# Stage seams in a seven-stage kernel: earlier loads for the next stage, and weights laid out transposed

## The chip, the cores and the metric

The kernel runs as one launch on one core of one Trainium2 chip. The metric is the device time of an execution in microseconds (us). Engines are named as in the profile: PE (matmul), PEld (weight load of PE), DVE, ACT, POOL, SP (here only a queue that issues DMAs).

## The reference, cut to what matters

Two layers over x of 2 x 1024 tokens of width 512. Each layer norms x, computes an attention branch s and a gate branch g, and sets x = x + s * g.

```python
x = L0_attn_x
xn = _layernorm(x)
s = L0_attn(xn)          # qkv, two causal convolutions on q and on k, l2 norm, rope,
                         # 16 heads of 64 over 4 kv heads, causal softmax, times w_o.T
g = silu(L0_ffn(xn))     # relu^2 mlp + routed latent path, layer norm
x = x + s * g
xn = _layernorm(x)
s = L1_attn(xn)          # wq, wk, wv; rope; 32 heads of 16 over 8 kv heads; each query keeps
                         # the first 128 keys, its last 128 keys and its 8 best chunks of 16; times wo.T
g = silu(L1_ffn(xn))     # 8 low-rank experts: softmax(xn @ Wr.T + br), A then B
x = x + s * g
```

## The kernel before, in words

The program is seven stages, one after another, each a block of hand-written instruction streams for the engines with counting semaphores between them: gate, project, query, attend, middle, select, finish. At the end of a block all engines meet, and SP has first waited for its last stores; no instruction of the next block starts before that. A stage that needs its inputs at once therefore pays for the loads that it issues at its own start. Intermediate tensors (`q_parts`, `k_high`, `k_low`, `v`, `o0T`, `x1`, `o1`, `g`, `g1`) go through DRAM.

**Query** (`query_phase`). PE convolves, per block m of 128 output channels (8 blocks) and per chunk n of 512 tokens (4 chunks), 72 matmuls out of `conv_in` (a kept SBUF tensor of 65,664 bytes per partition) with fp16 weight parts that ACT and DVE make from float32 rows: DVE finds the extremes of the rows (`extremes`, L1041 to L1044), PE turns and spreads the peak (`find_peak` L876, `share_peak` L881), DVE scales, ACT and DVE write `c_wT` (L923, L1067). The rows of block 0, `rows0`, were loaded in the project stage. At the stage's start SP issues the loads of `k_in` and `raw1`, of the rows of block 1, and of seven small tables (`k_mean`, bias, `head_sum`, `head_spread`, cos, sin, temp; L812 to L818). PE, ACT, DVE and POOL each begin by waiting for all seven (`wait_ge(tables, 16 * 7)`). A chain of norms, rotation and splitting runs beside the convolution for ten units (two of k, eight of q); "hooks" place its PE steps (`sums` L847, `turn`, `back`, `spread`) inside the convolution. Only `sums` onwards, ACT's `offsets` and POOL's `rotate` read the tables. The unit of the last block runs alone at the end, and its four stores (L829) end the stage.

**Attend** (`attend_phase`) is the first layer's attention: 16 pairs of heads p = (g, b, i), g a kv group, b the batch, i a pair in it. SP issues three small tables (the last is `temp`), then `load(0, b)` for both b (q 1 MB, k_high, k_low and v 256 KB each, for each b), then the weights of the middle stage as rows (`MiddleWeights.load`). PE waits for the tables and for the four loads of its b. SP later issues `load(g + 1, b)` when group g is done with its buffers, and `store(p)` of each pair's 512 KB to `o0T`. Buffers `q`, `k_high`, `k_low`, `v` are the stage's own.

**Middle** (`middle_phase`) first has a small block of its own (`prep`): SP issues the loads of chunk 0 (`o_in` 2 MB, `g_in` and `x_in` 1 MB each) and of cos, sin (4 x 512 KB) and `br`; PE turns the weight rows by transposes in 17 groups (L1510), ACT and DVE copy them out (L1518, L1526). Then the main block: `project(c)` (L1630, 64 matmuls a chunk, 4 chunks of 512 tokens), and the rest of the layer's projections.

**Select** is the second attention; SP stores each group's result to `o1` in halves (`store(g, half)`, L2050), 16 groups g = (j, u) with u the batch, and preloads the finish stage's weight rows, `g_in` and `x_in` of two chunks (`FinishInputs`).

**Finish** (`finish_phase`): SP issues the loads of `o_in` of chunks 0 and 1 (L2460), PE turns the weight rows (L2484), ACT copies them (L2521), PE turns the tokens (`turn`, L2494) and multiplies (`project`, L2503), DVE gates and adds, SP stores and loads the chunk after next.

Of the kernel before, what the change touches and what calls it, by code (L numbers as in the profile page):

```python
# [704 lines left out]
def query_phase(nc, sem, dram, ident, half, conv_in, unscale, rows0, rows0_loaded):  # L705

    with ExitStack() as ctx:
# [97 lines left out]
        def _(sp):  # L805
# [34 lines left out]
        def _(pe):  # L840
            def sums(j):

                pe.wait_ge(square_ready, j + 1)
                if j > 0:
                    pe.wait_ge(rnorm_ready, j)
# [60 lines left out]
            pe.wait_ge(tables, 16 * 7)  # L906
# [9 lines left out]
        def _(act):  # L916
# [39 lines left out]
            act.wait_ge(tables, 16 * 7)  # L956
            weights(0)
            squares(0)
            offsets(0)
# [63 lines left out]
        def _(dve):  # L1023
            dve.wait_ge(tables, 16 * 7)

# [114 lines left out]
def attend_phase(nc, sem, dram, ident_bf, mask_kq, weights):  # L1140

    with ExitStack() as ctx:
# [7 lines left out]
        q = [sb(f"q{b}", [P, G0, S], FP16) for b in range(B)]  # L1150
        k_high = [sb(f"k_high{b}", [P, S], FP16) for b in range(B)]
        k_low = [sb(f"k_low{b}", [P, S], FP16) for b in range(B)]
        v = [sb(f"v{b}", [P, QT, HD0]) for b in range(B)]
# [19 lines left out]
        loaded = [sem(f"d_loaded{b}") for b in range(B)]  # L1173
# [25 lines left out]
        def _(sp):  # L1199
# [4 lines left out]
            def load(g, b):  # L1204
                sp.dma_start(q[b][:], dram["q_parts"][g * G0:(g + 1) * G0, :, b * S:(b + 1) * S].rearrange("h p t -> p h t")).then_inc(loaded[b], 16)
                for to, name in ((k_high, "k_high"), (k_low, "k_low")):
                    sp.dma_start(to[b][:], dram[name][g, :, b * S:(b + 1) * S]).then_inc(loaded[b], 16)
                sp.dma_start(v[b][:], dram["v"][b * S:(b + 1) * S, g * HD0:(g + 1) * HD0].rearrange("(n p) c -> p n c", p=P)).then_inc(loaded[b], 16)

# [5 lines left out]
            for b in range(B):  # L1215
                load(0, b)
            weights.load(sp)
            for p in range(ALL):
                g, b, i = where(p)
                if i == G0 // 2 - 1 and g + 1 < KV0:  # L1220
                    sp.wait_ge(pv_done, QT * (p + 1))
                    load(g + 1, b)
                if p >= 1:
                    store(p - 1)
            store(ALL - 1)
# [185 lines left out]
class MiddleWeights:  # L1411


    def __init__(self, ctx, nc, dram, sem):
        def raw(name, shape):
            return ctx.enter_context(nc.sbuf_tensor(f"e_w_{name}", shape, F32))

        self.dram = dram
# [1271 lines left out]
```

## Time and profile before

| | |
|---|---|
| median of 3 runs | 2838.74 us (2836.09 to 2839.36) |
| profiled execution | 2833.69 us, its span 2831.9 us |
| PE busy | 2417.7 us, 85% of the span |
| DVE, ACT, POOL busy | 1246.7, 940.6, 749.5 us |
| granted PE clock, mean | 0.94 of full speed |
| read from HBM, written | 127.05 MB, 60.29 MB |

The span is that of the first to the last instruction of one profiled execution; the execution's own time is 1.8 us longer, and the median of the runs shown is 5.05 us above that. Times below are counted from the span's start. "Idle before" is how long an engine did nothing before an instruction, with what ended it.

### The profile page before, as it was taken

The page shows a single profiled execution, that of the slowest core. Times are in us where ns is not written, and L with a number is a line of the kernel's source. Part 1 is how long each engine was busy: PE and PEld are TensorE (multiplying, and loading weights), DVE is VectorE, ACT ScalarE, POOL GpSimd, SP SyncE. Part 2 cuts the span into 40 slices and gives each one's busy share as a digit, 9 for nine tenths or more (in the row PEclk, how much of TensorE's full clock was granted, in tenths as well). Part 3 has the DMA queues.
Part 4 walks back from the last instruction along what each step waited for, and adds up shares of the span by engine and source line. Part 5 has one row for each costly group of instructions (what it writes and reads, how often), then busy time and mean ns, then how long its engine had stood idle before and what let it go on. Part 6 is the DMA issues. An engine that isn't in the chain of part 4 may idle for free. (4 is left out here: it accounts for less than half of the span.)

```text
span 2831.9 us, 46056 instructions
## 1 busy us (share of the span) xinstructions
PE 2417.7 (85%) x19426; PEld 1159.1 (41%) x19426; DVE 1246.7 (44%) x2617; ACT 940.6 (33%) x1597; POOL 749.5 (26%) x749
## 2 busy tenths in 40 slices
PE   7999859999788999999499976888578888888766
PEld 3444334444333444443255543444233333333333
DVE  2332231100043333321287772444487877787602
ACT  1111120100021111110377750222257676767630
POOL 0111001110235222223344430222343333333300
PEclk9999979999889999999699988999789999999988
DMA  6000010000222111000422204331553553444122
GB/s 215 30 30 30 15 67 15 26 26 19 101 64 63 38 41 49 16 15 16 128 83 83 83 31 163 121 121 62 112 132 60 77 75 59 59 77 75 28 93 91
DMA packets 132462, 190.33 MB, mean 67 GB/s; under 512 B 45016, under 2 KB 67288, under 8 KB 130848
## 3 DMA queue, kind: packets, MB, share of 16 engines
q1 hardware_dynamic: 130144, 183.20, 24.8%
q8 instruction: 153, 2.51, 0.4%
q10 hardware_dynamic: 2112, 4.19, 0.4%
q14 instruction: 53, 0.43, 0.1%
HBM read 127.05 MB, written 60.29 MB: 66 GB/s over the span
## 5 line engine op out<-in xcount | busy, mean ns | idle before, releaser
L896 PE MATMUL c_ps_c<-conv_in,c_wT 128*128 128x512 f16 x2304 | 508.4, 380 | 2.6 <-DVE c_wT L1067 2.6
L2219 ACT ACTIVATE f_probs<-f_ps_s 128x512 f32<-128x512 f32 x576 | 321.5, 596 | 136.9 <-PE f_ps_s L2123 55.6
L2337 DVE TENSOR_REDUCE f_chunk_max<-f_ps_a 128x64 f32<-128x1024 f32 x320 | 321.8, 1033 | 92.1 <-PE f_ps_a L2090 50.8
L896 PEld LDWEIGHTS c_ps_c<-conv_in,c_wT 128*128 128x128 f16 x2304 | 222.6, 98 | 279.6 <-issue 13.5
L2123 PE MATMUL f_ps_s<-f_qs,f_ks 128*32 128x512 bf16 x2304 | 218.4, 387 | 64.1 <-ACT f_probs L2219 55.5
L2090 PE MATMUL f_ps_a<-f_ka,f_qa 128*32 128x512 bf16 (+3 forms) x3072 | 200.3, 339 | 47.1 <-DMA f_v_all<-v 21.4
L1325 ACT ACTIVATE d_probs<-d_ps_s,d_shift 128x512 f32<-128x512 f32 (+3 forms) x384 | 196.5, 583 | 82.5 <-PE d_ps_s L1264 72.8
L2145 PE MATMUL f_ps_o<-f_probs,f_v 128*32 128x512 f32 (+3 forms) x1536 | 151.8, 493 | 25.7 <-ACT f_probs L2219 25.6
L624 PE MATMUL b_ps<-b_xb,b_wT 128*128 128x512 f32 x320 | 140.5, 600 | 18.0 <-DMA b_xb<-xnT 18.0
L1259 PE MATMUL d_ps_s<-d_q,d_k_high 128*64 128x512 f16 (+3 forms) x768 | 125.7, 328 | 33.0 <-DMA d_v<-v 33.0
L1275 PE MATMUL d_ps_o<-d_probs,d_v 128*64 128x512 f32 (+3 forms) x768 | 146.0, 488 | 0.0
L2211 ACT ACTIVATE f_qs<-f_ps_t 32x512 bf16<-32x512 f32 x192 | 112.6, 586 | 100.2 <-PE f_ps_t L2105 97.3
L2090 PEld LDWEIGHTS f_ps_a<-f_ka,f_qa 128*32 128x32 bf16 x3072 | 75.5, 98 | 164.2 <-issue 61.9
L2277 POOL TENSOR_SCALAR f_absent<-f_rest 128x576 f32<-128x576 f32 x32 | 54.3, 1697 | 332.2 <-DVE f_rest L2354 332.2
L1630 PE MATMUL e_ps_s<-e_oT,e_o_in 128*128 128x512 f32 x256 | 115.7, 614 | 21.8 <-DMA e_x_in<-in_x 21.8
L2123 PEld LDWEIGHTS f_ps_s<-f_qs,f_ks 128*32 128x32 bf16 x2304 | 59.5, 96 | 163.7 <-ACT f_probs L2219 135.4
L1392 DVE RECIPROCAL d_inverse<-d_ps_n 128x1024 f32<-128x1024 f32 x16 | 104.9, 6558 | 44.7 <-PE d_ps_n L1286 44.7
L1264 PE MATMUL d_ps_s<-d_q,d_k_low 128*64 128x512 f16 (+3 forms) x384 | 124.3, 328 | 0.0
L1263 PE MATMUL d_ps_s<-d_q,d_k_low 128*64 128x512 f16 (+3 forms) x384 | 124.3, 328 | 0.0
L189 PE MATMUL a_ps_m<-a_xnT,a_up 128*128 128x512 f32 x256 | 112.3, 599 | 2.5 <-ACT a_relu L236 2.5
L207 PE MATMUL a_ps_d<-a_down,a_hidden 128*128 128x512 f32 x256 | 112.5, 592 | 0.0
L1032 DVE SCALAR_TENSOR_TENSOR c_raw<-c_ps_c,c_w_unscale,c_offset 128x512 f32<-128x512 f32 x32 | 24.0, 751 | 192.8 <-PE c_ps_c L896 192.8
(282 smaller groups left out, 3689.9 us busy)
## 6 DMA issues: line engine op xcount, KB each, us to landing
f_qa<-qk SPq DMA_DIRECT2D x96, 128.0 KB, 3.7
f_qs<-qk SPq DMA_DIRECT2D x96, 128.0 KB, 4.5
d_q<-q_parts SPq DMA_DIRECT2D x8, 1024.0 KB, 5.4
o0T<-d_stage SPq DMA_DIRECT2D x16, 512.0 KB, 2.6
e_o_in<-o0T SPq DMA_DIRECT2D x4, 2048.0 KB, 10.8
qk<-e_part SPq DMA_DIRECT2D x12, 640.0 KB, 4.9
rows<-in_qc_w SPq DMA_DIRECT2D x4, 1536.0 KB, 7.1
c_rows<-in_qc_w SPq DMA_DIRECT2D x4, 1536.0 KB, 7.7
```

Of the source, the lines that this page charges most:

```text
L624: last = pe.matmul(out[:], wT[:, k, u * P:(u + 1) * P], x[:, k, 1:], start=(k == 0), stop=(k == KD - 1))
L896: last = pe.matmul(ps_c[n % 2][:], wT[m % 2][:, w, i * TAPS + a, :], conv_in[:, x, i, b, h * CH + a:h * CH + a + CH], start=(i == 0 and a ...
L1259: pe.matmul(out[sides[e], lo - low:], k_high[b][:, keys[e]], q[b][:, h, lo:hi], start=True, stop=False)
L1263: pe.matmul(out[sides[0], lo - low:], k_low[b][:, keys[0]], q[b][:, h, lo:hi], start=False, stop=True)
L1264: pe.matmul(out[sides[1], lo - low:], k_low[b][:, keys[1]], q[b][:, h, lo:hi], start=False, stop=True)\
L1275: last = pe.matmul(ps_o[a * HD0:(a + 1) * HD0, lo:hi], v[b][:, kt, :], probs[n % RING][a][:, lo:hi], start=(kt == 0), stop=((kt + 1) * P = ...
L1325: act.activation(probs[n % RING][SCORES[c][1]][:, lo:hi], ps_s[c % BANKS][:, lo - hi + CH:], ACT.Exp, bias=shift[:, 0:1], scale=HD0 ** -0. ...
L2090: last = pe.matmul(out[side(e), h, 0:w], qa[u][:, 2 * p + h, side(e, qt * P)], ka[u][:, kh * CH:kh * CH + w], start=True, stop=not last_keys)
L2123: last = pe.matmul(out[side(e), :], ks[u][:, side(e, kt * P)], qs[u][version][:, :, at:at + P], start=True, stop=not (masked or part))
L2145: last = pe.matmul(ps_o[2 * HD1 * h:2 * HD1 * (h + 1), lo - half * CH:], v[u][:, kt, :], probs[m % HELD][:, h, lo - half * CH:], start=(kt ...
L2219: act.activation(probs[m % HELD][:, :, at:at + P], ps_s[n % 2][:].rearrange("p (h n) -> p h n", n=P), ACT.Exp, scale=HD1 ** -0.5).then_inc ...
L2337: dve.tensor_reduce(chunk_max[:, qt - 2, :, at:at + w // CHUNK], src.rearrange("p h (c k) -> p h c k", k=CHUNK), AX.X, ALU.max).then_inc(a ...
```

## The change: what it does

1. **Query stage, table waits.** DVE's wait for the seven tables is gone. PE waits for them in `sums(0)`, ACT after `weights(0)` and `squares(0)`. POOL waits as before.
2. **First attention's loads.** A new `AttendInputs` lays q, k_high, k_low, v of both b out in the first 28,672 bytes per partition of `conv_in`. In the query stage SP, at the last unit, waits for all convolutions and for the stores of the units before, issues the eight loads of group 0, and then stores the last unit. Attend issues none for group 0.
3. **Middle weights.** The host lays `w_o`, `wq`+`wk`, `wv`+`lora_a`+`lora_r`, `lora_b` out transposed. Attend's SP loads them straight into `oT`, `qkT`, `tokT`, `bT`, and cos, sin, `br` with them. The `prep` block, with its transposes and copies, is gone.
4. **Middle's first tokens.** `o_in`, `g_in`, `x_in` lie in another part of `conv_in`; attend's SP issues the loads of chunk 0 between the last but one and the last store, after a wait for the stores of pairs 0 to 13.
5. **Finish.** `wo` comes transposed by the host, the four groups of transposes and the copies are gone. The loads of `o1` for chunks 0 and 1 are issued in the select stage, in its last group before `store(g, 0)`, after a wait for all stores up to group 14.

```diff
@@ query_phase
                 if j + 2 < MQ:
                     sp.wait_ge(w_ready, PIECES * (j + 1))
                     load_rows(j + 2)
+                if j == UNITS - 1:
+                    sp.wait_ge(conv_done, NCH * MQ)
+                    sp.wait_ge(stored, stored_by(j))
+                    for b in range(B):
+                        attend_inputs.load(sp, 0, b)
                 store(j)
@@ sums
                 pe.wait_ge(square_ready, j + 1)
+                if j == 0:
+                    pe.wait_ge(tables, 16 * 7)
@@ tensor
-            pe.wait_ge(tables, 16 * 7)
             pe.wait_ge(cleared, 2)
@@ scalar
-            act.wait_ge(tables, 16 * 7)
             weights(0)
             squares(0)
+            act.wait_ge(tables, 16 * 7)
             offsets(0)
@@ vector
-            dve.wait_ge(tables, 16 * 7)
...
+class AttendInputs:
+    def __init__(self, dram, sem, space):
+        flat = space[:].rearrange("p a m b n -> p (a m b n)")
+        G0 = H0 // KV0
+        sizes = [G0 * S] * B + [S] * B + [S] * B + [2 * QT * HD0] * B
+        parts = [flat[:, sum(sizes[:i]):sum(sizes[:i + 1])] for i in range(len(sizes))]
...
+    def load(self, sp, g, b):
+        sp.dma_start(self.q[b], dram["q_parts"][g * G0:(g + 1) * G0, :, b * S:(b + 1) * S].rearrange("h p t -> p h t")).then_inc(self.loaded[b], 16)
+        for to, name in ((self.k_high, "k_high"), (self.k_low, "k_low")):
+            sp.dma_start(to[b], dram[name][g, :, b * S:(b + 1) * S]).then_inc(self.loaded[b], 16)
+        sp.dma_start(self.v[b], dram["v"][b * S:(b + 1) * S, g * HD0:(g + 1) * HD0].rearrange("(n p) c -> p n c", p=P)).then_inc(self.loaded[b], 16)
@@ attend_phase, sync
-            for b in range(B):
-                load(0, b)
             weights.load(sp)
             for p in range(ALL):
...
+            for i in range(2):
+                sp.wait_ge(stored[i], 16 * (ALL // 2 - 1))
+            weights.load_tokens(sp, 0)
             store(ALL - 1)
@@ MiddleWeights.load
-        sp.dma_start(self.o_rows[:], dram["w_o"].rearrange("(o p) c -> p o c", p=P)).then_inc(self.loaded, 16)
...
+        sp.dma_start(self.oT[:], dram["w_oT"].rearrange("(m p) d -> p m d", p=P)).then_inc(self.w_loaded, 16)
+        sp.dma_start(self.qkT[:].rearrange("p i k n -> p (i k n)"), dram["qk1_wT"]).then_inc(self.w_loaded, 16)
+        sp.dma_start(self.tokT[:].rearrange("p k t -> p (k t)"), dram["tok_wT"]).then_inc(self.w_loaded, 16)
+        sp.dma_start(self.bT[:], dram["lora_bT"]).then_inc(self.w_loaded, 16)
+        for b in range(B):
+            sp.dma_start(self.cos[:, b, :], dram["cos1"]).then_inc(self.tables, 16)
+            sp.dma_start(self.sin[:, b, :], dram["sin1"]).then_inc(self.tables, 16)
+        sp.dma_start(self.br[:], ...).then_inc(self.tables, 16)
+
+    def load_tokens(self, sp, c):
+        sp.dma_start(self.o_in, self.dram["o0T"][:, :, ds(c * CH, CH)].rearrange("m p t -> p m t")).then_inc(self.loaded, 16)
+        sp.dma_start(self.g_in, tokens("g")).then_inc(self.loaded, 16)
+        sp.dma_start(self.x_in, tokens("x")).then_inc(self.loaded, 16)
@@ middle_phase
-        with ExitStack() as prep:
...      (the whole prep block: loads of chunk 0 and of cos, sin, br; 17 groups of transposes; 17 copies)
@@ middle_phase, project
+                if c == 0:
+                    pe.wait_ge(weights.w_loaded, 64)
                 pe.wait_ge(loaded, 48 * (c + 1))
@@ select_phase, sync, in the loop over g
+                if g == GROUPS - 1:
+                    for half in range(2):
+                        sp.wait_ge(o_stored[half], 16 * (GROUPS - 1 + 1))
+                        inputs.load_heads(sp, half, half)
                 store(g, 0)
@@ FinishInputs, finish_phase
-        sp.dma_start(self.w_rows[:], self.dram["wo"].rearrange("(o p) c -> p o c", p=P)).then_inc(self.w_loaded, 16)
+        sp.dma_start(self.wT[:], self.dram["wo"].rearrange("(k p) d -> p k d", p=P)).then_inc(self.w_loaded, 16)
-            for u in range(2):
-                load(u, u)
-            for k in range(KO):
-                for o in range(D // P):
-                    last = pe.transpose(ps_t[k % 4][:, o * P:(o + 1) * P], w_rows[:, o, k * P:(k + 1) * P], ident[:])
-                last.then_inc(w_turned, 1)
-            for k in range(KO):
-                act.wait_ge(w_turned, k + 1)
-                act.activation(wT[:, k, :], ps_t[k % 4][:], ACT.Copy).then_inc(w_ready, 1)
```

## Rows read from the trace of the kernel before

**Rows 1.** The page's first part, busy time of PE and others.

```profile
PE 2417.7 (85%) x19426; PEld 1159.1 (41%) x19426; DVE 1246.7 (44%) x2617; ACT 940.6 (33%) x1597; POOL 749.5 (26%) x749
```

**Rows 2.** Waits of PE: us in total, times, longest us.

```profile
PE c_ps_x L876 <- DVE c_ends L1044: 38.7, 3, 28.2
PE d_ps_s L1259 <- DMA d_v<-v: 33.0, 1, 33.0
...
PE e_psw L1510 <- PEq L1142: 11.0, 1, 11.0
```

**Rows 3.** Timeline, project to query: start us, us, what [idle before].

```profile
761.61 0.20 POOL L985 MEMSET c_ones<- 1x128 f32 x1 [33.63 <-POOLq L384]
...
773.21 0.44 SPq L818 DMA_DIRECT2D c_temp<-in_key_temp  x1
779.38 3.35 DVE L1041 TENSOR_REDUCE c_ends<-rows 128x1 f32<-128x3072 f32 x1 [29.05 <-DMA c_temp<-in_key_temp]
...
790.47 9.89 PE L896 MATMUL c_ps_c<-conv_in,c_wT 128*128 128x512 f16 x36 [2.60 <-DVE c_wT L1067]
...
795.81 2.37 POOL L998 TENSOR_TENSOR c_turned<-c_k_in,c_cos 128x1024 f32<-128x1024 f32 x1 [33.42 <-DVE c_swapped L1076]
...
800.29 1.07 PE L847 MATMUL c_ps_n<-c_square,c_head_sum 128*32 128x512 f32 x8
```

**Rows 4.** Timeline, the first convolution block.

```profile
803.19 7.96 PE L896 MATMUL c_ps_c<-conv_in,c_wT 128*128 128x512 f16 x36
...
812.21 5.45 POOL L1007 TENSOR_TENSOR c_rnorm<-c_norm,half 128x32 f32<-128x32 f32 x1 [2.35 <-DVE c_norm L1080]
```

**Rows 5.** Timeline, query to attend.

```profile
1336.15 0.75 DVE L1032 SCALAR_TENSOR_TENSOR c_raw<-c_ps_c,c_w_unscale,c_offset 128x512 f32<-128x512 f32 x1 [12.62 <-PE c_ps_c L896]
...
1368.66 0.45 SPq L829 DMA_DIRECT2D q_parts<-c_high  x1
...
1376.15 0.42 SPq L1202 DMA_DIRECT2D d_temp<-in_key_temp  x1
...
1378.98 0.15 DVE L1354 TENSOR_SCALAR d_minus<-d_temp 128x1 f32<-128x1 f32 x1 [10.35 <-DMA d_temp<-in_key_temp]
...
1384.91 0.64 PE L1259 MATMUL d_ps_s<-d_q,d_k_high 128*64 128x512 f16 x2 [33.03 <-DMA d_v<-v]
```

**Rows 6.** Timeline, attend to middle.

```profile
1681.47 14.06 SPq L1213 DMA_DIRECT2D o0T<-d_stage  x2
...
1693.96 1.22 DVE L1397 TENSOR_TENSOR d_stage<-d_o_raw,d_inverse 128x1024 f32<-128x1024 f32 x1
1698.24 0.37 SPq L1470 DMA_DIRECT2D e_o_in<-o0T  x1
...
1698.30 5.67 PE L1510 MATMUL e_psw<-ident,e_w_o 128*128 128x128 f32 x32 [10.98 <-PEq L1142]
...
1711.55 29.43 PE L1630 MATMUL e_ps_s<-e_oT,e_o_in 128*128 128x512 f32 x64 [3.60 <-DMA e_x_in<-in_x]
```

**Rows 7.** The page's DMA issues: KB each, median us to landing.

```profile
o0T<-d_stage SPq DMA_DIRECT2D x16, 512.0 KB, 2.6
```

**Rows 8.** Timeline, middle's second chunk: a store and the loads behind it.

```profile
1742.46 0.38 SPq L1597 DMA_DIRECT2D x<-e_x  x1
...
1759.18 30.01 PE L1630 MATMUL e_ps_s<-e_oT,e_o_in 128*128 128x512 f32 x64 [18.20 <-DMA e_x_in<-in_x]
```

**Rows 9.** Timeline, select to finish.

```profile
2688.74 0.42 DVE L2382 TENSOR_TENSOR f_o_out<-f_ps_t,f_inverse 128x256 f32<-128x256 f32 x1
```

**Rows 10.** Timeline, start of the finish stage.

```profile
2721.69 3.65 PE L2484 MATMUL h_ps_t<-ident,h_w_rows 128*128 128x128 f32 x16 [3.47 <-PEq L1857]
...
2727.23 6.60 PE L2494 MATMUL h_ps_t<-ident,h_o_in 128*128 128x128 f32 x32 [1.90 <-DMA h_o_in<-o]
```

**Rows 11.** Windows: us, busy of PE, PEld, DVE, ACT, POOL, granted clock, DMA share, GB/s.

```profile
786.00:791.00 5.00, 1.69 (x6) 0.87 (x7) 2.43 (x7) 2.57 (x4) 0.00 (x0) 0.50 0.00 0
...
2730.00:2735.00 5.00, 5.00 (x25) 4.28 (x24) 0.00 (x0) 3.48 (x6) 0.00 (x0) 0.68 0.01 3
```

More of the change, by code:

```diff
@@ L702, in _, with query_phase @@
                         take(dve, b, h, u).then_inc(took_dve, 1)
-def query_phase(nc, sem, dram, ident, half, conv_in, unscale, rows0, rows0_loaded):
+def query_phase(nc, sem, dram, ident, half, conv_in, unscale, rows0, rows0_loaded, attend_inputs):
     with ExitStack() as ctx:
@@ L1149, in attend_phase @@
         LATE = S - KT_POOL * P
[L1150 to L1153, printed above, removed]
+        q, k_high, k_low, v, loaded, load = inputs.q, inputs.k_high, inputs.k_low, inputs.v, inputs.loaded, inputs.load
         ones = sb("ones", [P, HD0])
@@ L1411, with __init__, sb @@
 class MiddleWeights:
[L1414 to L1425 removed]
+    def __init__(self, ctx, nc, dram, sem, space, used):
+        def sb(name, shape):
+            return ctx.enter_context(nc.sbuf_tensor(f"e_{name}", shape, F32))
+        KV1D = KV1 * HD1
+        self.TOK = KV1D + HL * RL + HL
+        self.NQK = D // P + KV1D // P
+        flat = space[:].rearrange("p a m b n -> p (a m b n)")
+        sizes = [2 * MQ * CH, 2 * TT * D, 2 * TT * D]
+        o_in, g_in, x_in = [flat[:, used + sum(sizes[:i]):used + sum(sizes[:i + 1])].bitcast(F32) for i in range(3)]
+        self.dram = dram
+        self.o_in = o_in.rearrange("p (m t) -> p m t", t=CH)
+        self.g_in = g_in.rearrange("p (t d) -> p t d", d=D)
+        self.x_in = x_in.rearrange("p (t d) -> p t d", d=D)
+        self.oT = sb("oT", [P, MQ, D])
+        self.qkT = sb("qkT", [P, self.NQK, KD, P])
+        self.tokT = sb("tokT", [P, KD, self.TOK])
+        self.bT = sb("bT", [P, OL])
+        self.br = sb("br", [P, HL])
+        self.cos = sb("cos", [P, B, S])
+        self.sin = sb("sin", [P, B, S])
+        self.w_loaded = sem("e_w_loaded")
+        self.loaded = sem("e_loaded")
+        self.tables = sem("e_tables")
@@ L1462, in middle_phase @@
-        o_in = sb("o_in", [P, MQ, CH])
-        loaded = sem("e_loaded")
+        oT, qkT, tokT, bT, br, cos, sin = weights.oT, weights.qkT, weights.tokT, weights.bT, weights.br, weights.cos, weights.sin
+        o_in, g_in, x_in, loaded, load, tables = weights.o_in, weights.g_in, weights.x_in, weights.loaded, weights.load_tokens, weights.tables
         def tokens(name):
             return dram[name].rearrange("(c t p) d -> c p t d", t=TT, p=P)
-        def load(sp, c):
-            sp.dma_start(o_in[:], dram["o0T"][:, :, ds(c * CH, CH)].rearrange("m p t -> p m t")).then_inc(loaded, 16)
-            sp.dma_start(g_in[:], tokens("g")[ds(c, 1)].rearrange("a p t d -> p (a t) d")).then_inc(loaded, 16)
-            sp.dma_start(x_in[:], tokens("x")[ds(c, 1)].rearrange("a p t d -> p (a t) d")).then_inc(loaded, 16)
@@ L2435, in finish_phase @@
         KO = H1 * HD1 // P
-        w_rows, g_in, x_in, loaded = inputs.w_rows, inputs.g_in, inputs.x_in, inputs.loaded
-        wT = sb("wT", [P, KO, D])
-        o_in = [sb(f"o_in{i}", [P, TT, KO * P]) for i in range(2)]
+        wT, o_in, g_in, x_in, loaded = inputs.wT, inputs.o_in, inputs.g_in, inputs.x_in, inputs.loaded
         oT = [sb(f"oT{i}", [P, KO, CH]) for i in range(2)]
@@ L2458, in _ @@
         def _(sp):
-            def load(c, u):
-                sp.dma_start(o_in[u][:], tokens(dram["o1"])[ds(c, 1)].rearrange("a p t d -> p (a t) d")).then_inc(loaded[u], 16)
             def store(c, u):
```

127 lines of the change are left out of this document (36 added, 91 removed).

## The prediction

> **What bounds the kernel now.** I read the page first: PE is busy for 85% of the span [rows 1], no other engine for half of it. So inside a stage PE sets the pace, and 414 us are left in which it does nothing. The list of what PE waited for says where [rows 2]: long single waits, each at the start of a stage, and not many small ones. Every stage begins after all engines met, so such a wait shifts everything behind it and is paid in full. Then I read the timeline around each seam that the diff touches, to see which arrival ends the wait and what would end it if that arrival were gone. The gate stage and the seams gate to project and middle to select aren't touched. In a seam the test for each saved microsecond is: what is the next thing that PE has to wait for?
>
> **Seam 1, project to query.** The block opens at 761.61 (POOL's memset). DVE's first reduction starts at 779.38, released by the load of `temp`, the last of seven tables, issued at 773.21 [rows 3]. That reduction reads only `rows0`, which was loaded in the stage before. With the wait gone it starts with the block, at about 761.65: 779.38 - 761.65 = 17.7 us. From there the chain is the old one (two reductions, peak, scale, `c_wT`), 790.47 - 779.38 = 11.1 us long, and PE's first convolution starts at 772.8 instead of 790.47.
>
> Who still needs the tables? They land at 779.4 as before, since SP's queue is the same there. PE meets them in `sums(0)`, which stood 800.29 - 790.47 = 9.8 us behind the first convolution [rows 3], so at 782.6: 3.2 us after they land. It doesn't wait. ACT waits before `offsets(0)` from some 776 to 779.4; the offsets are needed by DVE's `take(0, 0)` only after 72 matmuls. Queued behind that wait is `sums_out(0)`, which can't start before `sums(0)` is done anyway. POOL's `rotate(0)` started at 795.81, i.e. would start at 778.1, and now starts at 779.4, 1.3 us late against PE. Behind it is POOL's `invert(0)`, before which POOL sat idle for 2.35 us [rows 4]; the 1.3 us go into that. So nothing of 17.7 is given back. The early squares on ACT need only `k_in` and `raw1`, issued first.
>
> PE starts cold either way: the granted clock is 0.50 at 786 to 791 [rows 11], that is 1.2 GHz, and its idle stretch only shrinks from some 32 to some 15 us. Were the clock to stay up I would gain what separates the first 36 matmuls, 9.89 us [rows 3], from the next 36, 7.96 us [rows 4]: 1.9 us. I count nothing and keep it for the upper bound. Seam 1: **17.7 us, 16.5 to 19.6**.
>
> **Seam 2, query to attend.** The last convolution ends at 1336.1 and the last unit's chain of ACT, DVE, POOL and small PE steps runs to 1368.66, where its stores start [rows 5]. The eight new loads are issued when the convolution is done; SP has nothing else to do for those 32 us, and 3.5 MB need some 12 us at the rate of seam 3. They are long there when the block ends. The wait for stores of earlier units holds nothing up, for these stores belong to a unit whose chain ran during the last block of convolutions. The tail itself isn't shortened: it is bound by its chain. In the new block PE waited for `v`'s load to 1384.91; the next thing it needs is the three tables, and DVE's first instruction shows that `temp`, the last, is there at 1378.98 [rows 5]. Saving: 1384.91 - 1378.98 = **5.9 us, 5.4 to 6.5**. ACT's table load and first exponential hang on PE's first score and move with it. The weights of the middle stage are now 4 MB of longer runs and 2 MB of cos and sin, on SP's queue from 1376.6; nobody reads them for 300 us, and SP's next duty, `load(1, 0)`, comes after a pair's values, some 40 us later. Nothing.
>
> **Seam 3, attend to middle.** PE began the middle stage at 1698.30 with the transposes and reached `project(0)` at 1711.55, released by the load of `x_in` [rows 6]. Removed: 68 transposes, 17 copies, one meeting of the engines, and the wait for 4 MB. If tokens and weights are there, `project(0)` takes the place of the transposes at 1698.30: 13.25 us.
>
> But the token loads are 4 MB, issued after `store(14)` at 1681.47 [rows 6], and `store(15)` is issued behind them. DVE's last product starts at 1693.96 and takes 1.22 us [rows 6], so `store(15)` is issued at 1695.2. Do the loads get out of its way? The nearest row: behind a 1 MB store issued at 1742.46, the same three loads released PE at 1759.18 [rows 8], so 5 MB in 16.7 us, 300 GB/s with the start-up in it. Here 0.5 + 4 MB = 4.7 million bytes need 15.7 us, from 1681.5 to 1697.2. A store to `o0T` lands 2.6 us after its issue [rows 7], so `store(15)` at 1697.8; with 0.5 MB behind the loads it lands at 1697.2 + 1.7 = 1698.9. The seam ends 1.1 us later (bounds: 0 if the loads run faster, 4 if they run at 250 GB/s). A second small loss: PE enters `project(0)` after 11 us of idleness, where it had warmed up in the transposes. The 64 matmuls took 29.43 us there and 30.01 us after an 18 us wait [rows 6, 8]: 0.6 us. Seam 3: 13.25 - 1.1 - 0.6 = **11.6 us, 8.5 to 13.3**. After it the middle stage is the old one: its chunks load each other through the same queue and the same single buffers.
>
> Here a rule of the Trainium skill speaks against the change, "DMA: Bandwidth & Descriptors", section "Queues, rings and completion order": each DMA engine takes descriptors in ring order, and the copies of one issuing engine share those rings, so a store issued behind 4 MB of loads waits for them. No row of before has a store behind loads with its landing in view. The Trainium skill's table in the same page's section "Bandwidth" has 16 MB at 425 GB/s; as an estimate from that Trainium skill page 4.7 million bytes would be through in 11.1 us, before `store(15)` is issued, and the 1.1 us would be nothing (total 41.8 instead of 40.7).
>
> **Seam 4, select to finish.** The half `(14, 1)` is written by DVE at 2688.74 [rows 9], stored right away, and landed some 2.6 us later; then the two loads of `o1`, 2 MB, have 30 us until the finish stage. Queued behind SP's new wait are the two last stores, whose data come 10 us and more later. So they aren't held up. The finish stage starts at 2721.69 with PE's transposes of weights; `turn(0)` started at 2727.23, released by the load of `o_in` [rows 10]. It takes their place: 2727.23 - 2721.69 = **5.5 us, 4.5 to 6**. PE is cold in either case (clock 0.68 for 2730 to 2735, rising some 6 us after the turns began [rows 11]), so the turns take their 6.6 us again. From there each chunk waits for the store and loads of the one before, as now. The four copies on ACT (L2521) lay beside PE: nothing.
>
> **Sum.** 17.7 + 5.9 + 11.6 + 5.5 = 40.7 us, against the profiled execution 2833.69 - 40.7 = 2793.0 us (span 2791.2). The median of the runs shown is 5.05 us above the profiled execution, and the result is a median too: 2838.74 - 40.7 = **2798.0 us**.
>
> **Rivals.**
>
> *Rival A, the token loads eat their own gain.* Loads and `store(15)` share one queue; if the loads run at half the 300 GB/s (they read `o0T` in 1024 runs of 2 KB while DMA also writes), they land at 1713, later than now: seam 3 costs 2 us, total 27, time 2811.7. Against it: the same loads, with a larger store in front, ran at 300 [rows 8]. 5%. The Trainium skill's ring-order rule, "DMA: Bandwidth & Descriptors", "Queues, rings and completion order", is the same mechanism for the store behind them.
>
> *Rival B, a second wait in the query stage takes the place of the first.* In the first block PE already waited three times for DVE's extremes, 38.7 us in all, of which 28.2 are the seam [rows 2]. If the early start leaves ACT or POOL, which still wait for the tables, on the chain that feeds the second and third extremes, up to the 3.4 us (ACT) or 1.3 us (POOL) come back, and if rows of block 1, landing about 770 to 774, were late for DVE, a little more. With 3.4 us given back the total is 37.3, the time 2801.4. 12%.
>
> *Rival C, a larger gain:* the clock stays up or rises sooner at the seams now that PE idles less (seam 1 by 1.9, seam 3 by 2), total 44.6, time 2794.1. For it: shorter idle stretches. Against it: the shortest of them, before the finish stage, is 3.5 us [rows 10] and the clock there is low [rows 11]. 10%.
>
> *Rival D, the other side: the attention loop gets slower.* Its q, k, v now lie in `conv_in`, at other addresses, from which PE reads every score and value. The loop lasts 1698.3 - 1384.9 = 313 us with PE busy nearly throughout. From 13% longer PE instructions on (40.7 / 313) it takes all the gain back; at 16%, 50 us, the time would be 2848. For it: nothing that the trace shows; no row tells an operand's address. 2%.
>
> *Rival E, the loads are hidden anyway,* that is, the inferred releasers are wrong and the seams are set by the meeting of engines: then seams 1 and 4 give 0 and the total is 17.5, time 2821.2. Against it: POOL runs at the block's opening, 17.7 us before DVE, and PE transposes 5.5 us before its turn. 3%.
>
> **How the numbers follow.** The forecast with its bounds has 68%, A 5, B 12, C 10, D 2, E 3. The four seams' bounds add up to 34.9 and 45.4 us: 2803.8 and 2793.3. They hardly all fall on one side, but the runs themselves spread by 2.7 us below and 0.6 above their median, and a median of another set can move as much. I take 2789 to 2808, which also holds B and C and leaves out A, D and E, 10%, and some of the rest. A measurement of this kernel can tell a change from none at about 0.2%, 5.7 us. Only D ends slower: 2%, and 1 more for the unforeseen; within 0.2%: 1%; faster: 96%.
>
> **What would show it.** Right: DVE's first reduction of the query stage at the block's opening, and PE's first convolution 11 us later; no wait of PE at the first `sums`; PE's first score of attend some 3.7 us after the block's first POOL instruction, released by `temp`'s tables; `project(0)` of the middle stage within 2 us of the block's opening, the block itself opening 1.1 us later after DVE's last product than now (4.3 us); `turn(0)` as PE's first work in the finish stage. Wrong: the third wait for extremes in the query stage longer than now; attend's loop not 313 us; the span from the last product to `project(0)` above 8 us.

## The result, and the profile after

The changed kernel takes 2793.87 us (median of 4 executions, 2788.19 to 2863.77), the kernel before 2837.58 us in the same set: 43.7 us less, ratio 0.9839 with a 95% interval of 0.9814 to 0.9864. One of the four executions, the one of 2863.77 us, ran at a lower granted clock (0.902, the others 0.941 to 0.948) and is left out of the ratio, and the median of the other three is 2789.5 us, 48.1 less and only just inside the forecast range. Forecast were 2798.0 us, 40.7 us less, in a range of 2789 to 2808. A later set of five runs of the same kernel gave 2793.95 us against 2837.69 us, ratio 0.9846 (0.9833 to 0.986). The profiled execution took 2789.5 us, its span is 2787.7 us.

First the busy times from the page of the changed kernel.

```profile
PE 2398.0 (86%) x19342; PEld 1143.3 (41%) x19342; DVE 1241.4 (45%) x2609; ACT 932.8 (33%) x1584; POOL 750.5 (27%) x749
```

PE is busy for 19.7 us less [rows 1]: 13.3 us of that are the 68 + 16 transposes that are gone. The other 6.4 lie mostly in stages that the change doesn't touch, and are scatter: a second profile of the same kernel has PE busy for 2405.9 us. The span is 44.2 us shorter, so somewhat more than half of it was idle time of PE. The list of PE's waits says which (us in total, times, longest us):

```profile
PE h_ps_t L2451 <- DMA h_o_in<-o: 29.0, 2, 14.5
...
PE d_ps_s L1278 <- DMA d_temp<-in_key_temp: 27.0, 1, 27.0
...
PE c_ps_x L883 <- DVE c_ends L1048: 20.9, 3, 10.5
...
PE e_ps_s L1595 <- DMA conv_in<-in_x: 17.2, 1, 17.2
...
PE e_ps_s L1595 <- DVEq L55: 11.2, 1, 11.2
...
PE h_ps_t L2451 <- ACTq L55: 3.6, 1, 3.6
```

Against [rows 2]: the wait for DVE's extremes fell by 17.8 us, and PE's first score of attend is released by `temp` and no longer by `v`. Two releasers are new, `DVEq L55` and `ACTq L55`: L55 is the line of `primed`, with which an engine opens a stage (it sets the semaphores' starting values). At these two seams PE now waits for nothing but the opening of the stage. The two 14.5 us waits inside finish stayed, and so did the wait for chunk 1 in middle, 17.2 us (18.2 before).

The timeline of the changed kernel at the first seam:

```profile
759.20 0.20 POOL L991 MEMSET c_ones<- 1x128 f32 x1 [33.62 <-POOLq L384]
759.24 3.35 DVE L1045 TENSOR_REDUCE c_ends<-rows 128x1 f32<-128x3072 f32 x1 [11.31 <-PEq L384]
...
770.27 10.49 PE L903 MATMUL c_ps_c<-conv_in,c_wT 128*128 128x512 f16 x36 [2.54 <-DVE c_wT L1071]
...
778.38 2.38 POOL L1004 TENSOR_TENSOR c_turned<-c_k_in,c_cos 128x1024 f32<-128x1024 f32 x1 [18.39 <-DMA c_temp<-in_key_temp]
...
780.69 1.06 PE L854 MATMUL c_ps_n<-c_square,c_head_sum 128*32 128x512 f32 x8
...
792.48 5.45 POOL L1013 TENSOR_TENSOR c_rnorm<-c_norm,half 128x32 f32<-128x32 f32 x1
```

DVE starts 0.04 us after the block opens, where it started 17.77 us after [rows 3]. PE's first `sums` shows no wait. POOL's 2.35 us of idleness before `invert(0)` [rows 4] is gone. Counted from DVE's first reduction, `rotate(0)` starts 19.14 us behind it instead of 16.43, so 2.7 us late, and `invert(0)` 33.24 instead of 32.83: the idleness took up all but 0.4 us. At the other three seams:

```profile
1316.79 0.38 SPq L1162 DMA_DIRECT2D conv_in<-q_parts  x1
...
1359.31 0.64 PE L1278 MATMUL d_ps_s<-conv_in 128*64 128x512 f16 x2 [26.99 <-DMA d_temp<-in_key_temp]
...
1655.93 0.32 SPq L1231 DMA_DIRECT2D o0T<-d_stage  x1
...
1656.36 0.37 SPq L1473 DMA_DIRECT2D conv_in<-o0T  x1
...
1668.42 1.22 DVE L1416 TENSOR_TENSOR d_stage<-d_o_raw,d_inverse 128x1024 f32<-128x1024 f32 x1
1669.67 0.33 SPq L1231 DMA_DIRECT2D o0T<-d_stage  x1
1672.93 29.51 PE L1595 MATMUL e_ps_s<-e_oT,conv_in 128*128 128x512 f32 x64 [11.15 <-DVEq L55]
...
2680.84 0.42 DVE L2351 TENSOR_TENSOR f_o_out<-f_ps_t,f_inverse 128x256 f32<-128x256 f32 x1
...
2684.06 5.07 PE L2451 MATMUL h_ps_t<-ident,h_o_in 128*128 128x128 f32 x32 [3.62 <-ACTq L55]
```

`project(0)` follows DVE's last product by 4.51 us, where the transposes followed it by 4.34 and `project(0)` by 17.59 [rows 6]. `turn(0)` follows DVE's last output of select by 3.22 us. Laid end to end, the two profiles give this ledger (a piece is the difference of two starts):

| piece | before | after | gain |
|---|---|---|---|
| to the opening of query (nothing changed there) | 761.61 | 759.20 | 2.41 |
| opening to DVE's first reduction | 17.77 | 0.04 | 17.73 |
| to the end of the convolution | 556.77 | 557.55 | -0.78 |
| tail of query to the opening of attend | 39.15 | 38.97 | 0.18 |
| opening to PE's first score | 9.61 | 3.55 | 6.06 |
| attention loop to DVE's last product | 309.05 | 309.11 | -0.06 |
| last product to `project(0)` | 17.59 | 4.51 | 13.08 |
| middle and select to DVE's last output | 1007.07 | 1007.91 | -0.84 |
| last output to `turn(0)` | 8.61 | 3.22 | 5.39 |
| turns, products, the rest | 104.67 | 103.64 | 1.03 |

The sum is 44.2 us, the difference of the spans. The four seams hold 42.3 of it. The first line is luck of that execution: over the 13 profiles of this study the query block opened between 759.2 and 764.5 us, the stretch from DVE's first reduction to the end of the convolution lasts 556.8 to 559.6 us, and the line of middle and select lies between 1004.3 and 1014.6 us in the twelve of them that load middle's chunks as these two kernels do. That is why the experiments are read seam by seam, from starts inside one profile, and only then by their times.

### The profile page after: what moved, and what is told of

The parts are those of the page before. It is cut to its first block and busy times, and to the rows that moved or that the text cites. A ratio compares the mean times of both kernels' runs of the same rounds, so it can differ in the third digit from the quotient of the medians.

```text
span 2787.7 us, 45851 instructions
## 1 busy us (share of the span) xinstructions
PE 2398.0 (86%) x19342; PEld 1143.3 (41%) x19342; DVE 1241.4 (45%) x2609; ACT 932.8 (33%) x1584; POOL 750.5 (27%) x749
## 5 line engine op out<-in xcount | busy, mean ns | idle before, releaser
L1278 PE MATMUL d_ps_s<-conv_in 128*64 128x512 f16 (+3 forms) x768 | 125.6, 329 | 27.0 <-DMA d_temp<-in_key_temp 27.0
L2180 ACT ACTIVATE f_qs<-f_ps_t 32x512 bf16<-32x512 f32 x192 | 112.7, 587 | 103.8 <-PE f_ps_t L2074 101.0
L1294 PE MATMUL d_ps_o<-d_probs,conv_in 128*64 128x512 f32 (+3 forms) x768 | 146.0, 488 | 0.0
L1595 PE MATMUL e_ps_s<-e_oT,conv_in 128*128 128x512 f32 x256 | 115.9, 615 | 28.3 <-DMA conv_in<-in_x 17.2
L1282 PE MATMUL d_ps_s<-conv_in 128*64 128x512 f16 (+3 forms) x384 | 124.2, 328 | 0.0
L1283 PE MATMUL d_ps_s<-conv_in 128*64 128x512 f16 (+3 forms) x384 | 124.2, 328 | 0.0
```

The lines of the kernel that those rows point to most:

```text
L1278: pe.matmul(out[sides[e], lo - low:], k_high[b][:, keys[e]], q[b][:, h, lo:hi], start=True, stop=False)
L1282: pe.matmul(out[sides[0], lo - low:], k_low[b][:, keys[0]], q[b][:, h, lo:hi], start=False, stop=True)
L1283: pe.matmul(out[sides[1], lo - low:], k_low[b][:, keys[1]], q[b][:, h, lo:hi], start=False, stop=True)\
L1294: last = pe.matmul(ps_o[a * HD0:(a + 1) * HD0, lo:hi], v[b][:, kt, :], probs[n % RING][a][:, lo:hi], start=(kt == 0), stop=((kt + 1) * P = ...
```

## The experiments

Each is the changed kernel with one edit undone, unless it says otherwise. Reference values are those of the changed kernel: 2793.95 us in its second set.

### The table waits undone

```diff
+            pe.wait_ge(tables, 16 * 7)     # head of PE's stream; the one in sums(0) is gone
+            act.wait_ge(tables, 16 * 7)    # ahead of weights(0)
+            dve.wait_ge(tables, 16 * 7)    # head of DVE's stream
```

> The changed kernel with one part undone: PE, ACT and DVE wait for the seven tables at the head of the query stage again. My theory (the seam's gain is the wait for the last table and nothing else): from the block's opening to DVE's first reduction 17.8 us instead of 0.04, everything behind it as late, time 17.7 us above the changed kernel, about 2811.5 us. Rival (part of the gain was luck of the run or a shorter warm-up of PE after the shorter idle stretch): 15 to 16 us, the convolution's first 36 matmuls faster or slower than 10.5 us.

Measured: 2813.65 us (median of 4), ratio to the kernel before 0.992 (0.9905 to 0.9935), 19.7 us above the changed kernel. The timeline at DVE's first reduction and PE's first convolution; the block opened at 762.60:

```profile
780.16 3.35 DVE L1046 TENSOR_REDUCE c_ends<-rows 128x1 f32<-128x3072 f32 x1 [28.83 <-DMA c_temp<-in_key_temp]
...
791.25 9.63 PE L901 MATMUL c_ps_c<-conv_in,c_wT 128*128 128x512 f16 x36 [2.60 <-DVE c_wT L1072]
```

17.56 us are back, released by `temp`. The first 36 matmuls take 9.63 us after the long idle stretch and 10.49 after the short one: the start isn't warmer (9.85 to 10.57 us in the ten profiles with the short stretch, 9.63 to 10.28 in the three with the long one). The theory stands: the wait is back at nearly its full length and not at the rival's 15 to 16 us. That the matmuls differ from 10.5 us, as the rival had it, has the sign opposite to a warm-up. The medians differ by 2.2 us more than the seam (19.7 against 17.5), which the scatter of the untouched stretches covers: the span of this profile is 17.2 us above that of the second profile of the changed kernel (2811.8 and 2794.6 us).

### Attend's loads of group 0 back in attend

```diff
-                if j == UNITS - 1:           # query: wait, then attend_inputs.load(sp, 0, b)
...
+            for b in range(B):               # attend, before weights.load(sp)
+                load(sp, 0, b)
```

> The changed kernel with the eight loads of group 0 issued by SP at the head of the attend stage again, still into the space of conv_in. My theory: PE's first score comes 9.6 us after POOL's first instruction of the block instead of 3.55, released by v's load; 6.1 us more, about 2800 us; the attention loop itself lasts 313.4 us as in both kernels. Rival (the place of q, k and v in conv_in matters to PE): the loop's length differs between kernels with and without it; this run has it in conv_in, and its loop would then differ from the one of before.

Measured: 2800.72 us, 6.8 us above the changed kernel; ratio to before 0.988 (0.9863 to 0.9896). The block opened at 1360.72:

```profile
1371.07 0.64 PE L1275 MATMUL d_ps_s<-conv_in 128*64 128x512 f16 x2 [33.78 <-DMA conv_in<-v]
```

10.35 us from the opening, 6.8 more than in the changed kernel. The loop from PE's first score to DVE's last product takes 309.10 us here and lies between 309.04 and 309.13 in all 13 profiles, two of which (the kernel before and the one with tokens only) have q, k and v in buffers of their own. Where PE reads them from makes no difference.

### Seam 3, its two halves apart

Tokens late, weights transposed:

```diff
-            weights.load_tokens(sp, 0)       # attend, before the last store
...
+            load(sp, 0)                      # middle, SP's first instruction
             store_x1(0)
```

> The changed kernel with the token loads of chunk 0 issued at the head of the middle stage; weights still arrive transposed, so there is no prep block. Theory T (the token loads set the seam, the transposes lay hidden under them): project(0) starts 12 to 13.5 us after the stage opens, the whole 13.1 us of seam 3 are lost, about 2806 us. Theory W (the transposes set the seam, the loads only their last 3.6 us): about 4 us are lost, 2798 us.

The kernel before with tokens early, weights as rows:

```diff
+            for i in range(2):               # attend, before the last store
+                sp.wait_ge(stored[i], 16 * (ALL // 2 - 1))
+            weights.load_tokens(sp, 0)
             store(ALL - 1)
...
-                    load(sp, 0)              # prep block of middle
```

> The kernel before with one thing changed: o_in, g_in and x_in of chunk 0 are loaded into buffers of their own by SP between the last but one and the last store of attend; rows of weights, prep block, transposes and copies as before, cos, sin and br at the head of the middle stage. Theory T, with the transposes next in line (9.7 us of PE plus the meeting at the block's end): project(0) starts about 10.5 to 11 us after the stage opens instead of 13.25, gain 2.5 us against before, 2835 us. Theory W' (loads are all of it, the transposes cost nothing even uncovered): gain 13 us, 2824.5 us. If T holds here and in the run with late tokens, neither half of seam 3's edit earns it alone.

Measured: 2809.95 us for the first, 16.0 above the changed kernel; 2831.87 us for the second, against 2836.27 us of the kernel before in the same set, ratio 0.9982 (0.9973 to 0.9991). `project(0)` in the one and in the other; DVE's last products began at 1673.32 and 1694.88:

```profile
1690.59 29.69 PE L1593 MATMUL e_ps_s<-e_oT,conv_in 128*128 128x512 f32 x64 [23.90 <-DMA conv_in<-in_x]
```

```profile
1710.30 27.70 PE L1635 MATMUL e_ps_s<-e_oT,e_w_o_in 128*128 128x512 f32 x64 [1.09 <-DVEq L55]
```

| from DVE's last product to `project(0)` | tokens at the stage's head | tokens early |
|---|---|---|
| weights as rows | 17.59 (before) | 15.42 |
| weights transposed | 17.27 | 4.51 (changed) |

The transposed weights alone are worth 0.3 us, the early tokens alone 2.2 us, both 13.1 us. The seam is a maximum of two arms of nearly equal length, not a sum. With the tokens alone early, `project(0)` itself is shorter as well: 27.70 us, 1.09 us behind the transposes, against 29.43 in the kernel before. So that edit alone is worth 3.9 us in the profile and 4.4 by the medians. The first run's median is 16.0 us above the changed kernel where the seam says 12.8; in its profile middle and select took 1013.4 us (1007.9 and 1009.8 in the two profiles of the changed kernel), which is scatter.

### The order of the token loads and the last store

```diff
+            sp.wait_ge(o_used, ALL)          # loads held until the last product is done
             weights.load_tokens(sp, 0)
             store(ALL - 1)
```

> The changed kernel with SP's token loads held until DVE's last product of attend is done, so that the 4 MB are issued right before the last store instead of 13 us before it. Theory R (the store goes through the same rings behind the loads): the engines meet only when the store has landed behind them, project(0) starts about 15.5 us after DVE's last product began (4.5 us in the changed kernel) and is released by the meeting of the engines. Rival I (the store is not held by the loads ahead of it): the stage opens about 6.5 us after that product began and PE then waits for the load of x_in, to about 13.8 us, released by that load. By the Trainium skill, DMA: Bandwidth & Descriptors, Queues, rings and completion order, R holds.

```diff
+            store(ALL - 1)                   # the store first
             weights.load_tokens(sp, 0)
-            store(ALL - 1)
```

> The changed kernel with the last store of attend issued first and the token loads right behind it. By both theories of the order the store lands as in the kernel before, the stage opens about 4.5 us after DVE's last product began, and PE waits for x_in until about 14 us. If theory R holds, this order is some 1.5 us better than the loads just before the store; by rival I it is equal or slightly worse. Time about 10 us above the changed kernel.

One execution each: 2807.03 and 2809.68 us. The loads just before the store (DVE's last product at 1672.11), then the store first (product at 1669.95):

```profile
1673.42 0.37 SPq L1474 DMA_DIRECT2D conv_in<-o0T  x1
...
1675.02 3.12 SPq L1231 DMA_DIRECT2D o0T<-d_stage  x1
1689.28 11.21 PE L1596 MATMUL e_ps_s<-e_oT,conv_in 128*128 128x512 f32 x20 [23.81 <-DVEq L55]
```

```profile
1671.63 0.37 SPq L1473 DMA_DIRECT2D conv_in<-o0T  x1
...
1686.43 14.10 PE L1595 MATMUL e_ps_s<-e_oT,conv_in 128*128 128x512 f32 x26 [23.12 <-DMA conv_in<-in_x]
```

With the loads ahead, the stage opens only 17.17 us after the product began, and PE goes on with the opening. The 512 KB store was issued 1.7 us later than in the changed kernel (2.91 us after the product began, behind three issues of loads) and landed 13.5 us after its issue, where 2.6 is the rule [rows 7]: together 12.6 of the 12.7 us by which the seam is longer. With the store ahead, PE waits for `x_in` to 16.48 us. The releasers are those of theory R. The two lengths were expected 1.7 and 2.5 us too short, and the second order is better by 0.7 us at the seam, not by 1.5; the times of the two single executions stand the other way round, because middle and select took 1014.6 us in the second and 1009.1 in the first. The Trainium skill, "DMA: Bandwidth & Descriptors", "Queues, rings and completion order", says that each DMA engine takes a ring's descriptors in order; these two runs agree, with 17.17 us and an opening that waits for the store.

### Seam 4, its two halves apart

Heads late, `wo` transposed; then `wo` as rows, heads early:

```diff
-                        inputs.load_heads(sp, half, half)   # select, last group
...
+                inputs.load_heads(sp, u, u)                 # finish, SP's first instructions
```

> The changed kernel with the loads of o1 for chunks 0 and 1 at the head of the finish stage again; wo still arrives transposed. From DVE's last output of select to turn(0): 3.2 us in the changed kernel, 8.6 in the one before. Theory (the o_in load alone sets this seam): 8.6 here, all 5.5 us lost. Rival (the weight transposes set it): 5 or less.

```diff
+            for k in range(KO):              # finish, PE, ahead of turn(0); copies on ACT too
+                for o in range(D // P):
+                    last = pe.transpose(ps_t[k % 4][:, o * P:(o + 1) * P], inputs.w_rows[:, o, k * P:(k + 1) * P], ident[:])
```

> The changed kernel with wo loaded as rows and turned by PE at the head of the finish stage again; the heads are loaded in the select stage. Theory: the transposes, hidden before under the load of o_in, are now on the path: 3.65 us of PE and about 0.7 us for ACT's last copy, so turn(0) comes 7.6 us after DVE's last output of select, 4.3 us later than in the changed kernel and 1.0 us earlier than in the kernel before. As for the clock: in the changed kernel the 32 transposes of turn(0) and turn(1) took 5.07 us against 6.60 before, without a gap ahead of them; here with nearly no gap behind the weight transposes they should take at most 4.5 us. Rival (nothing lost, the transposes cost nothing): 3.2 us and 5.1 us.

One execution each: 2801.07 and 2795.45 us. `turn(0)` in the first (DVE's last output of select at 2686.03), and the weight transposes and `turn(0)` in the second (output at 2685.28):

```profile
2694.50 6.66 PE L2449 MATMUL h_ps_t<-ident,h_o_in 128*128 128x128 f32 x32 [8.86 <-DMA h_o_in<-o]
```

```profile
2688.34 3.41 PE L2452 MATMUL h_ps_t<-ident,h_w_rows 128*128 128x128 f32 x16 [3.46 <-PEq L1822]
...
2692.48 3.69 PE L2462 MATMUL h_ps_t<-ident,h_o_in 128*128 128x128 f32 x32 [0.73 <-issue]
```

Heads late: 8.47 us instead of 3.22, nearly all of the seam's gain lost. Rows back: `turn(0)` at 7.20 us, 4.0 later than in the changed kernel, but its 32 transposes take 3.69 us and not 5.07. Up to the first product (4.91 us after `turn(0)` in the changed kernel, 3.52 here) the loss is 2.6 us. In this one profile, weight transposes that run right ahead of the turns shorten them; in the kernel before, a wait of 1.90 us lay between the two [rows 10].

### The changed kernel again, and two steps further

> The changed kernel once more, unchanged, for the size of the gain and for what varies from run to run. By the ten profiles so far the query block opened at 759.2 to 764.1 us, though nothing ahead of it differs, so a single profile places the end to some 5 us only. Expected: median 2794 to 2797 us, ratio 0.985; seam lengths within 0.3 us of the first profile: 0.04 us to DVE's first reduction, 3.6 us to PE's first score, 4.5 us from the last product to project(0), 3.2 us from DVE's last output of select to turn(0).

Measured: 2793.95 us (2792.17 to 2796.37). The seams, in order, are 0.04, 3.74, 4.52 and 3.21 us, as expected; the query block opened at 764.51 us, 5.3 us later than in the first profile.

Two waits of 14.5 us in finish and one of 17.2 in middle are of the same kind: a load that is issued later than its buffer is free. In finish the heads of chunks 2 and 3 get a semaphore of their own and are issued when PE has turned chunks 0 and 1:

```diff
+                    sp.wait_ge(t_done, KO * (2 * i + u + 1))
+                    inputs.load_heads(sp, 2 * i + 2 + u, u)
+                for u in range(2):
                     store(2 * i + u, u)
                     inputs.load(sp, 2 * i + 2 + u, u)
-                    inputs.load_heads(sp, 2 * i + 2 + u, u)
```

> The changed kernel, and in the finish stage the loads of o1 for chunks 2 and 3 hang on PE having turned chunks 0 and 1 (their buffers are free then), with a semaphore of their own, instead of on the stores of chunks 0 and 1. Theory (the two waits of 14.5 us in the finish stage are the same kind of seam, a load issued later than its buffer is free): both waits go, the turns and products behind them run at the full clock, 29 + 4.5 us less, about 2761 us. Rival (the load only moves the wait to DVE, which needs g_in and x_in of chunks 2 and 3, still loaded after the stores): DVE waits for them, gain 20 us or less, 2775 us.

Middle, on top of it: two sets of `o_in`, `g_in`, `x_in` in `conv_in`, one semaphore for each.

```diff
+            load(sp, 1)
             store_x1(0)
-            load(sp, 1)
+            load(sp, 2)
             for c in range(NCH - 2):
                 store_x1(c + 1)
-                load(sp, c + 2)
+                if c + 3 < NCH:
+                    load(sp, c + 3)
                 store_rest(c)
```

> The kernel with the finish stage's heads loaded by turn, and in the middle stage two sets of o_in, g_in, x_in in the space of conv_in (the second where q, k and v were), so that chunk 1 is loaded while project(0) runs and chunk c + 2 after the adds of chunk c. Theory: the 17.2 us wait before project(1) goes, and some 2 us of slow clock behind it, 19 us less than the kernel with the heads alone, about 2742 us. Rival (project(1) then waits for DVE's norm of chunk 0, whose x1 store and reciprocal work now lie beside it): 8 to 12 us less, 2751 us.

Measured: 2761.09 us, ratio to before 0.9729 (0.9713 to 0.9744), and 2738.61 us, ratio 0.9652 (0.9639 to 0.9665). The finish stage of the first, from SP's early loads on, and the first two projections of middle in the second:

```profile
2695.38 2.84 SPq L2400 DMA_DIRECT2D h_o_in<-o  x2
...
2697.66 13.90 PE L2465 MATMUL h_ps_y<-h_wT,h_oT 128*128 128x512 f32 x32
...
2711.40 1.91 PE L2454 MATMUL h_ps_t<-ident,h_o_in 128*128 128x128 f32 x16
...
2713.15 13.90 PE L2465 MATMUL h_ps_y<-h_wT,h_oT 128*128 128x512 f32 x32
```

```profile
1674.88 56.75 PE L1600 MATMUL e_ps_s<-e_oT,conv_in 128*128 128x512 f32 x128 [11.16 <-DVEq L55]
```

PE turns chunk 2 in 1.91 us without a wait, where it waited 14.5 us and then took 3.68. From the first product of finish to the end the kernel needs 64.74 us instead of 98.73, so 34.0 us less (33.5 were expected). In middle, 128 matmuls run in one piece of 56.75 us, where 64 + 64 with the wait between them took 76.7. The second run is 22.5 us below the first (19 expected). Both theories hold, and neither rival. The last kernel takes 99 us less than the one before the change, 55 less than the changed one.

## Why the prediction was right, point by point

**What bounds.** Right: PE and, at the seams, what it waits for. Undoing an edit brought its wait back each time, with the releaser that was read from the trace of before.

**Seam 1.** Forecast 17.7 us, measured 17.73; undone, 17.56. One step was wrong without a price: the tables did not land "as before". `temp` was issued 11.6 us after the opening in both kernels, but landed 7.5 us after its issue instead of 6.2, so POOL's `rotate(0)` could start only 19.2 us after the opening. The early start also brings SP's next load forward, the 1.5 MB of rows of block 2:

```profile
770.76 0.44 SPq L818 DMA_DIRECT2D c_temp<-in_key_temp  x1
773.03 0.33 SPq L807 DMA_DIRECT2D rows<-in_qc_w  x1
```

In the kernel before it was issued 20 us behind `temp`, now 2.3. In all ten profiles with the early start `temp` takes 7.3 to 7.7 us to land, in the three with the late one 6.1 to 6.2; no run takes that load out by itself. PE's `sums` still came 2.3 us behind the tables (3.2 forecast), and POOL's lateness, 2.7 us and not 1.3, went into its 2.35 us of idleness but for 0.4. Rival B didn't happen: PE's two other waits for the extremes sum to 10.4 us as against 10.5 before. The query stage behind the first reduction is 0.8 us longer, which is within its scatter. The warmer start of the upper bound and of Rival C had the wrong sign.

**Seam 2.** Forecast 5.9, measured 6.06 and, in the second profile, 5.87; undone, 6.8. `temp` is the new limit, as argued. Rival D fell: the loop is the same to 0.1 us.

**Seam 3.** Forecast 11.6, measured 13.08. The step that was mis-sized is the delay of `store(15)`: 1.1 us forecast, 0.17 measured (4.51 - 4.34). Part of it is a slip of units: the 5 MB of [rows 8] are 5.24 million bytes, so their 16.7 us are 314 GB/s, while the 4.7 to which the 300 was applied are already in millions. At 314 the loads end 0.7 us earlier and the delay is 0.4. Here the windows around the loads, in the changed kernel, with granted clock, DMA share and GB/s at the end, say

```profile
1656.00:1662.00 6.00, 3.68 (x8) 0.77 (x8) 1.97 (x3) 0.00 (x0) 0.63 (x2) 0.51 0.86 264
1662.00:1668.00 6.00, 0.00 (x0) 0.00 (x0) 6.00 (x1) 0.00 (x0) 0.00 (x0) 0.50 1.05 408
1668.00:1672.00 4.00, 0.00 (x0) 0.00 (x0) 1.61 (x2) 0.00 (x0) 0.00 (x0) 0.50 0.76 303
```

that 4.0 million bytes had moved by 1668, and the remaining 0.7 million of the loads need 1.7 us at 408 GB/s: by this estimate they were through at about 1669.7, just as `store(15)` was issued at 1669.67. By the trace `x_in`, issued at 1657.86, landed 12.6 us later, at 1670.5, and the store 2.6 us after its issue, as in the kernel before [rows 7]. In the second profile the overlap is larger:

```profile
1663.07 0.64 SPq L1475 DMA_DIRECT2D conv_in<-in_x  x1
...
1674.88 0.33 SPq L1231 DMA_DIRECT2D o0T<-d_stage  x1
```

`x_in` took 13.1 us there and landed 1.3 us after the store was issued, and still the store landed after 2.6 us. So besides the rate, the price of such a short overlap was too high: it cost nothing. The 11.1 us that the prediction gave as its other estimate for the same bytes are too short, since the last load landed 14.6 us after `store(14)` was issued. The mechanism was right, as the two orders of loads and store show; the change escapes it because 13 us lie between the two issues and the loads need nearly all of them.

The second term, 0.6 us of slower clock in `project(0)`, wasn't there: 29.51 us against 29.43, and 29.2 to 29.6 in other profiles with early tokens and transposed weights. The reading "it had warmed up in the transposes" was wrong for `project(0)`. In the kernel before, the 3.60 us wait for `x_in` came between them, and the granted clock, 0.98 from 1702 to 1712, fell again:

```profile
1712.00:1716.00 4.00, 4.00 (x7) 1.60 (x6) 0.00 (x0) 0.00 (x0) 0.00 (x0) 0.58 1.01 396
```

Where only 1.09 us lay between, in the run with tokens only, the same 64 matmuls took 27.70 us. Rival A needed half the rate and is out.

**Seam 4.** Forecast 5.5, measured 5.39. But the turns "take their 6.6 us again" was wrong: 5.07 and 5.92 us in the two profiles of the changed kernel. With early heads and no weight transposes ahead the 32 transposes take 5.07 to 6.12 us in nine profiles, right behind the weight transposes 3.69 in one. The windows of the changed kernel there:

```profile
2684.00:2686.00 2.00, 1.94 (x9) 1.97 (x10) 0.00 (x0) 0.60 (x1) 0.00 (x0) 0.50 0.00 0
2686.00:2688.00 2.00, 2.00 (x16) 2.00 (x16) 0.00 (x0) 1.71 (x4) 0.00 (x0) 0.77 0.00 0
2688.00:2692.00 4.00, 4.00 (x19) 2.33 (x18) 0.00 (x0) 1.99 (x5) 0.00 (x0) 1.00 0.00 0
```

The clock is at its upper level (2.4 GHz) some 3 us after the turns began, where it had risen some 6 us after them [rows 11]. From `turn(0)` to the end the gain is 1.0 to 1.2 us, which would be a part of Rival C. But it isn't shown to come from the edit. The run with tokens only has the finish stage of the kernel before, with heads late and the weight transposes, and its turns were short too:

```profile
2728.39 5.15 PE L2499 MATMUL h_ps_t<-ident,h_o_in 128*128 128x128 f32 x32 [1.71 <-DMA h_o_in<-o]
```

From there to the end it needs 103.8 us, against 104.7 in the kernel before, 104.8 with only the heads late, and 103.3 to 103.8 in the seven profiles with this stage as the change has it. Why the clock rises sooner in one execution than in another, 2.9 to 5.0 us after `turn(0)` in profiles where the stage begins alike, stays open.

**The sum.** 42.3 us at the seams, 40.7 forecast; nearly all of the difference is seam 3. The medians say 43.7, with an interval that reaches from 39 to 53 us in the first set (ratios 0.9864 and 0.9814) and from 40 to 47 in the second. What lies between 42.3 and 43.7 isn't told from the scatter of the untouched stages, and neither is the total better known than to a few us: of the 4.1 us by which the time undercuts the forecast, 1.2 are the kernel before, whose median was 2837.58 us in this set and 2838.74 in the forecast. Rival E is out: seams 1 and 4, to which it gave nothing, gave 17.7 and 5.4 us.

## What to carry to other kernels

Before two edits of a seam are priced, price each arm that ends there: here the loads and the transposes were within 2 us of each other, so each edit alone was worth 0.3 and 2.2 us at the seam, and both 13.1. Loads issued ahead of a store in the same queue should be nearly through when the store is issued: 1.3 us of overlap cost nothing here, but with 4 MB issued 1.6 us ahead the store, and with it the meeting of all engines, came some 11 us later. Ask, too, what else an earlier start sets off: here the next load of rows went out 17.8 us earlier, and the last table landed 1.3 us later. Look for every load that is issued later than its buffer comes free, inside the stages as well: three such places left in the changed kernel gave 55 us, more than the four seams.

## What the runs showed of the hardware that was not expected

A shorter idle stretch of PE (11 us instead of 28) before the query stage didn't make its start warmer: the first 36 matmuls took 10.49 and 10.53 us in the two profiles of the changed kernel and 9.89 in the one before, and in two of the ten profiles with the short stretch the next 36 were slow as well (9.64 us; 7.96 in all others); why stays open. And work that is useless on the path can still pay a part of its price: in one profile, 16 transposes ahead of 32 others cost 4.0 us and gave 1.4 back in the turns behind them (3.69 against 5.07 us; 2.2 against the second profile's 5.92). In another, `project(0)` took 27.70 us 1.09 us behind the transposes of the weights, and 29.2 to 29.6 as the first work of the stage.
